# Attention's projections of the second batch and the values placed between the first score blocks, and another order and shape of the stack loads

## The reference, cut to what matters

```python
def _L0_attn_ref(x, w_qkv, w_out, b_out):          # x: (2, 1024, 256)
    qkv = (x @ w_qkv.T).reshape(B, S, 3, H, D)      # H = 16 heads, D = 16
    q, k, v = jnp.moveaxis(qkv, 2, 0)
    ...
    out = _flash_attention_v2(q, k, v, BLOCK_SIZE, scale)   # blocks of 128 keys, their own maxima
    return out.transpose(0, 2, 1, 3).reshape(B, S, E) @ w_out.T + b_out
```

## Time and profile before

| what | value |
|---|---|
| median of 3 runs | 1293.59 us (1291.06 to 1298.01) |
| the profiled execution, its own time | 1297.3 us |
| its span, first to last instruction | 1295.6 us |
| busy PE / DVE / ACT / POOL | 87% / 64% / 49% / 46% |
| mean granted clock of PE | 0.95 of full |
| DMA | 137.21 MB, mean 106 GB/s |

### The profile page before, as it was taken

How to read it: one execution, slowest core, us unless ns; L and a number is a source line. 1 busy time by engine, 2 the same in 40 slices (tenths; PEclk the granted TensorE clock), 3 DMA queues, 4 the chain that set the end, 5 groups by cost and what they waited for, 6 DMA issues and landing times. The chain is left out here.

```text
span 1295.6 us, 21119 instructions
## 1 busy us (share of the span) xinstructions
PE 1128.8 (87%) x6374; PEld 660.5 (51%) x6374; DVE 825.3 (64%) x1537; ACT 633.3 (49%) x1320; POOL 592.2 (46%) x589
## 2 busy tenths in 40 slices
PE   5489999999999995888898977897999998999965
PEld 2152222222222223455753556356888886788854
DVE  6399999999999945665454556897333333222246
ACT  1126777777777781455313342221555554444471
POOL 7000355667345363576541102458544457555521
PEclk8888999999999997999989997899899999999989
DMA  4990234234130104000000000210689888788877
GB/s 135 152 228 14 47 59 64 28 41 61 27 44 13 13 9 171 0 2 1 1 3 1 1 1 10 89 56 26 197 242 242 238 238 252 241 267 255 261 253 253
DMA packets 128383, 137.21 MB, mean 106 GB/s; under 512 B 47430, under 2 KB 99366, under 8 KB 128207
## 3 DMA queue, kind: packets, MB, share of 16 engines
q1 hardware_dynamic: 118783, 110.42, 34.2%
q0 software_dynamic: 9216, 25.18, 6.1%
q10 hardware_dynamic: 272, 0.26, 0.1%
HBM read 109.06 MB, written 24.12 MB: 103 GB/s over the span
## 5 line engine op out<-in xcount | busy, mean ns | idle before, releaser
L495 ACT ACTIVATE l_ret_store<-attn_st 128x512 f32<-128x512 f32 x512 | 280.1, 598 | 103.1 <-PE attn_st L406 93.3
L519 DVE TENSOR_REDUCE attn_neg<-attn_mx 128x8 f32<-128x1024 f32 x256 | 299.2, 1202 | 12.9 <-PE attn_mx L386 11.9
L2010 DVE SCALAR_TENSOR_TENSOR exp_sums<-exp_y_ps,moe_mask,exp_sums 128x256 f32 x159 | 77.0, 484 | 202.8 <-PE exp_y_ps L1921 97.3
L406 PE MATMUL attn_st<-attn_q_st,attn_k_st 128*128 128x512 bf16 x512 | 173.9, 384 | 2.8 <-ACT l_ret_store L495 2.1
L1912 PE MATMUL exp_h_ps<-keep_prod,moe_w 128*88 128x128 f32 x1272 | 169.9, 277 | 7.1 <-DMA moe_w<-in_w 5.2
L386 PE MATMUL attn_mx<-attn_k_st,attn_q_st 96*128 96x512 bf16 x512 | 156.2, 387 | 14.5 <-DVE attn_neg L519 14.2
L1912 PEld LDWEIGHTS exp_h_ps<-keep_prod,moe_w 128*88 128x88 f32 x1272 | 147.8, 158 | 23.6 <-DMA moe_w<-in_w 12.2
L418 PE MATMUL attn_o<-l_ret_store,l_ret_tab 128*32 128x512 f32 x1024 | 136.4, 604 | 0.8 <-ACT l_ret_store L495 0.8
L1874 POOL DMA_INDIRECT y_rows<-exp_sums,moe_dst_i x96 | 93.7, 976 | 82.9 <-DVE exp_sums L2010 75.6
L406 PEld LDWEIGHTS attn_st<-attn_q_st,attn_k_st 128*128 128x128 bf16 x512 | 48.3, 97 | 155.9 <-ACT l_ret_store L495 114.6
L1966 ACT ACTIVATE moe_ht<-exp_h_ps 88x256 f32<-88x256 f32 x159 | 60.4, 380 | 95.6 <-PE exp_h_ps L1912 95.5
(11 more groups left out here) (317 smaller groups left out, 1921.0 us busy)
## 6 DMA issues: line engine op xcount, KB each, us to landing
moe_w<-in_w SPq DMA_DIRECT2D x254, 176.0 KB
keep_prod<-in_w SPq DMA_DIRECT2D x64, 176.0 KB
exp_tiles<-y_rows SPq DMA_DIRECT2D x11, 768.0 KB, 10.3
parts<-l0b_front SPq DMA_DIRECT2D x32, 192.0 KB, 10.6
attn_k_st<-parts SPq DMA_DIRECT2D x48, 128.0 KB, 7.1
attn_q_st<-parts SPq DMA_DIRECT2D x48, 128.0 KB, 7.7
l_ret_tab<-in_tables SPq DMA_DIRECT2D x4, 1024.0 KB
exp_sums<-y_rows SPq DMA_DIRECT2D x5, 768.0 KB, 10.5
```

Of the source, the lines that this page charges most:

```text
L406: pe.matmul(st_ps[n % BANKS][:], k_st[g % BUFS][:, h, kt * P:(kt + 1) * P], q_st[g % BUFS][:, h, c * CH:(c + 1) * CH], start=True, stop=Tr ...
L495: act.activation(probs[s % 2][:, h], st_ps[n % BANKS][:], ACT.Exp, scale=SCALE0).then_inc(exp_done, 1)
L519: dve.tensor_reduce(neg[m % 2][:, i], mx_ps[slot["score", n] % 2][:].rearrange("p (j k) -> p j k", k=P), AX.X, ALU.max, negate=True).then_ ...
L2010: dve.scalar_tensor_tensor(out=sums[:, bass.ds(at, 1)], in0=y_ps[b % 2][:, 0:E].unsqueeze(1), scalar=mask[:, b:b + 1], in1=sums[:, bass.ds ...
```

## The change

Part by part:

1. **PAIRS is reordered**, so that the key parts of the six pairs read 0, 1, 2, 0, 1, 0. RUNS names the three runs of consecutive key parts, and `load_stack` loads them with three transfers of 48, 32 and 16 rows. The columns of `w_qk` are reordered on the host so that a group's 64 channels are ordered dimension by head; a stack row is then one run of 8 KB in DRAM for all four heads. The queries still take six transfers of 16 rows, now after the keys. Nine transfers replace twelve.
2. **Order on PE, DVE and ACT.** Only the eight blocks of batch 0 (EARLY) come first. Then eight rounds follow: scores 2i and 2i+1, block 8+i, values 2i and 2i+1. DVE does two reduces and one split a round. The three banks are dealt in the order of use (`uses`, `bank_of`).
3. **SP's queue.** Stack 0 is loaded after save 4, the copies of the marks go out after save 7, stack 1 after save 9, and stack 2 behind `place_neg(0)`, `place_wj(0)`, x and the bias. `w_v` is loaded by SP after `x_t`, no longer by ACT at the start.
4. **POOL's constants.** The marks are made first, and for one head alone (32 x 1024 instead of 32 x 4096); three transfers spread them over the other heads and stacks instead of two. The memset of `v_st` writes only the half that is not overwritten, and comes later.

The diff, cut:

```diff
-PAIRS = ((0, 0), (0, 1), (1, 0), (1, 1), (0, 2), (2, 0))
+PAIRS = ((0, 0), (0, 1), (0, 2), (1, 0), (1, 1), (2, 0))
+RUNS = ((0, 3), (3, 2), (5, 1))
...
+        EARLY = 8
+        ROUNDS = len(blocks) - EARLY
+        values = [range(NT * i // ROUNDS, NT * (i + 1) // ROUNDS) for i in range(ROUNDS)]
+        uses = [("block", n) for n in range(EARLY)]
+        for i in range(ROUNDS):
+            uses += [("block", EARLY + i)] + [("value", t) for t in values[i]]
+        bank_of = {use: n % BANKS for n, use in enumerate(uses)}
...
+                for j, count in RUNS:
+                    rows = slice(D0 * j, D0 * (j + count))
+                    qp, kp = PAIRS[j]
+                    sp.dma_start(k_st[g % BUFS][rows], a["parts"][g, 1, kp:kp + count].rearrange("a (d h) t -> (a d) h t", h=G0)
+                                 ).then_inc(stack[g % BUFS], 16)
                 for j, (qp, kp) in enumerate(PAIRS):
-                    rows = slice(D0 * j, D0 * j + D0)
-                    sp.dma_start(k_st[g % BUFS][rows], a["parts"][g, 1, kp].rearrange("(h d) t -> d h t", d=D0)
-                                 ).then_inc(stack[g % BUFS], 16)
-                    sp.dma_start(q_st[g % BUFS][rows], a["parts"][g, 0, qp].rearrange("(h d) t -> d h t", d=D0)
+                    sp.dma_start(q_st[g % BUFS][D0 * j:D0 * (j + 1)], a["parts"][g, 0, qp].rearrange("(d h) t -> d h t", h=G0)
                                  ).then_inc(stack[g % BUFS], 16)
...
+            sp.dma_start(w_v[:], a["w_v"].rearrange("(k p) n -> p k n", p=P)).then_inc(v_weights, 16)
             for n in range(len(blocks)):
                 save(n)
-                if n == 3:
+                if n == 4:
                     load_stack(0)
-                if n == 5:
+                if n == EARLY - 1:
+                    sp.wait_ge(ready, 1 + PARTS)
+                    sp.dma_start(k_st[0][STACK:P, 1:G0], k_st[0][STACK:P, 0:1].to_broadcast([P - STACK, G0 - 1, SEQ])
+                                 ).then_inc(marked, 16)
+                    for i in range(1, BUFS):
+                        sp.dma_start(k_st[i][STACK:P], k_st[0][STACK:P, 0:1].to_broadcast([P - STACK, G0, SEQ])
+                                     ).then_inc(marked, 16)
+                if n == EARLY + 1:
                     load_stack(1)
-                if n == 11:
-                    load_stack(2)
-            sp.wait_ge(ready, 10)
-            for i in range(1, BUFS):
-                sp.dma_start(k_st[i][STACK:P], k_st[0][STACK:P]).then_inc(marked, 16)
+            place_neg(0)
+            place_wj(0)
             sp.dma_start(x[:], a["x"].rearrange("(t p) n -> p t n", p=P)).then_inc(x_in, 16)
             sp.dma_start(bias[:], a["b_out"].partition_broadcast(P)).then_inc(x_in, 16)
-            place_neg(0)
-            place_wj(0)
+            load_stack(2)
...
-            ordered(pool.memset(v_st, 1.0))
+            marks = k_st[0][STACK:P, 0].rearrange("r (j k) -> r j k", k=P)
...
+            ordered(pool.memset(v_st.rearrange("p b k h d -> p (b k h) d")[:, :, D0:2 * D0], 1.0))
...
-            for n in range(len(blocks)):
+            for n in range(EARLY):
                 project(n)
             pe.wait_ge(v_weights, 16)
-            for t in range(NT):
-                project_v(t)
-                score(t)
+            for i in range(ROUNDS):
+                score(2 * i)
+                score(2 * i + 1)
+                project(EARLY + i)
+                for t in values[i]:
+                    project_v(t)
...
-            act.dma_start(w_v[:], a["w_v"].rearrange("(k p) n -> p k n", p=P)).then_inc(v_weights, 16)
...
-            for n in range(NB):
+            for n in range(EARLY):
+                split_block(n)
+            for i in range(ROUNDS):
+                reduce(2 * i)
+                reduce(2 * i + 1)
+                split_block(EARLY + i)
```

More of the change, by code:

```diff
@@ L133, in attend @@
         saves = {n: n // SLOTS + 1 for n in range(len(blocks))}
+        EARLY = 8
[5 more added lines that the diff above has]
+        bank_of = {use: n % BANKS for n, use in enumerate(uses)}
+        order_of = {use: n for n, use in enumerate(uses)}
         ring, slot = [], {}
@@ L255, in ordered @@
                 pool.wait_ge(ready, done)
-            ordered(pool.memset(v_st, 1.0))
+            marks = k_st[0][STACK:P, 0].rearrange("r (j k) -> r j k", k=P)
+            ordered(pool.memset(marks, 0.0))
+            for part in range(PARTS):
+                ordered(pool.affine_select(out=marks, in_=marks, compare_op=ALU.not_equal, fill=1.0,
+                                           base=-KTS * part, pattern=[[-1, KTS], [0, P]], channel_multiplier=1))
             for m in (ident_bf, ident):
@@ L347, in _, with free_use @@
         def _(pe):
+            def free_use(kind, n):
+                r = order_of[kind, n] - BANKS
+                if r >= 0:
+                    was, m = uses[r]
+                    pe.wait_ge(rest_done if was == "block" else v_kept, m + 1)
             def project(n):
@@ L358, in project_v @@
             def project_v(t):
-                n = len(blocks) + t
-                if t < BANKS:
-                    pe.wait_ge(rest_done, n - BANKS + 1)
-                else:
-                    pe.wait_ge(v_kept, t - BANKS + 1)
+                free_use("value", t)
                 for k in range(KT):
-                    mm = pe.matmul(st_ps[n % BANKS][:, 0:E], x_t[:, k, t * P:(t + 1) * P], w_v[:, k, :],
+                    mm = pe.matmul(st_ps[bank_of["value", t]][:, 0:E], x_t[:, k, t * P:(t + 1) * P], w_v[:, k, :],
                                    start=(k == 0), stop=(k == KT - 1))
@@ L422, in _ @@
             pe.wait_ge(weights, 16)
[L423 removed]
+            for n in range(EARLY):
                 project(n)
             pe.wait_ge(v_weights, 16)
[L426 to L428 removed]
+            for i in range(ROUNDS):
[4 more added lines that the diff above has]
+                    project_v(t)
+            for n in range(2 * ROUNDS, NB + 2):
+                score(n)
             pe.wait_ge(ready, 11)
[L430 to L431 removed]
             turn_neg(0)
@@ L457, in _ @@
         def _(act):
-            act.dma_start(w_v[:], a["w_v"].rearrange("(k p) n -> p k n", p=P)).then_inc(v_weights, 16)
-            for n in range(len(blocks)):
-                act.wait_ge(projected, n + 1)
-                if n >= SLOTS:
-                    act.wait_ge(saved[n % SLOTS], 32 * saves[n - SLOTS])
-                act.activation(parts[:, n % SLOTS, 0], st_ps[n % BANKS][:], ACT.Copy).then_inc(high_done, 1)
-            act.wait_ge(ready, 1)
-            for t in range(NT):
-                act.wait_ge(v_done, t + 1)
-                act.activation(v_st[:, t // KTS, t % KTS, :, 0:D0],
-                               st_ps[(len(blocks) + t) % BANKS][:, 0:E].rearrange("p (h d) -> p h d", d=D0),
-                               ACT.Copy).then_inc(v_kept, 1)
+            for kind, n in uses:
+                bank = st_ps[bank_of[kind, n]]
+                if kind == "block":
+                    act.wait_ge(projected, n + 1)
+                    if n >= SLOTS:
+                        act.wait_ge(saved[n % SLOTS], 32 * saves[n - SLOTS])
+                    act.activation(parts[:, n % SLOTS, 0], bank[:], ACT.Copy).then_inc(high_done, 1)
+                else:
+                    act.wait_ge(ready, 2 + PARTS + 4)
+                    act.wait_ge(v_done, n + 1)
+                    act.activation(v_st[:, n // KTS, n % KTS, :, 0:D0], bank[:, 0:E].rearrange("p (h d) -> p h d", d=D0),
+                                   ACT.Copy).then_inc(v_kept, 1)
             def keep_neg(m):
@@ L502, in _, with split_block @@
         def _(dve):
-            for n in range(len(blocks)):
+            def split_block(n):
                 dve.wait_ge(high_done, n + 1)
-                dve.tensor_tensor(rest[:, n % 2], st_ps[n % BANKS][:], parts[:, n % SLOTS, 0],
+                dve.tensor_tensor(rest[:, n % 2], st_ps[bank_of["block", n]][:], parts[:, n % SLOTS, 0],
                                   ALU.subtract).then_inc(rest_done, 1)
@@ L544, in invert_total @@
                 dve.reciprocal(total[u % 2][:], total[u % 2][:]).then_inc(inverted, 1)
-            for n in range(NB):
+            for n in range(EARLY):
[4 more added lines that the diff above has]
+                split_block(EARLY + i)
+            for n in range(2 * ROUNDS, NB):
                 reduce(n)
@@ L2120, in lay_out @@
     w = np.asarray(i["L0_attn_w_qkv"])
-    d["w_qk"], d["w_v"] = t(w[:2 * E]), t(w[2 * E:])
+    d["w_qk"], d["w_v"] = t(w[:2 * E].reshape(2 * GROUPS // BATCH, G0, D0, E).swapaxes(1, 2).reshape(2 * E, E)), t(w[2 * E:])
     w = t(np.asarray(i["L0_attn_w_out"])).reshape(KT, 2, G0, D0, E)
```

18 lines of the change are left out of this document (5 added, 13 removed).

## The result

The changed kernel takes 1272.16 us (median of 4 runs, 1270.73 to 1277.06) against 1292.32 before (4 runs, 1287.66 to 1298.01): ratio 0.984, 95% interval 0.9807 to 0.9874. The forecast was 1274.6 with a range of 1269.5 to 1284.5. The profiled span fell from 1295.6 to 1274.1, by 21.5 us.

The account below looks back on a forecast made before the run. DVE bounds attention's loop, so only its start counts: 35.7 + 34.4 + 2.4 + 1.1 + 8.9 = 82.5, 19.0 us earlier than 101.5. From a median of 1293.6 that gives 1274.6 us, range 1269.5 to 1284.5.

Parts of the forecast that it names:

- Bound and rigid rest: Attention's main loop, bound by DVE, and the 837 us behind it move rigidly with the loop's start, 19.0 us earlier.
- Blocks 0 to 3 and POOL: Before the loop: smaller marks on POOL end 10.0 us of DVE stalls; stack 0 issued at 22.9 to 23.0, not 33.2.
- Moving w_v: At the start: w_v no longer shares the DMA with w_qk and the first x_t; 0.5 us taken, bounds 0 to 0.8.
- Stack 0: Stack 0's load: 2.0 us, queries 6.4 and keys 4.3 after issue at 23.0, so scores start at 35.7.
- Rounds: Eight rounds paced by PE at 4.3 us, 34.4 in all, plus 2.4 for PE's restart at its lower clock.
- What hides: Slots for blocks 11 to 15, stack 1 and the marks' transfers are all in time: cost 0.
- the tail of the queue: SP's queue: x, bias and stack 2 finish before place_neg(1) is needed; cost 0, bounds 0 to 3 us.
- D: Rival: PE never gets its full clock in the rounds, loop starts at 114.5, slower than before at 1306.6 us; chance 0.03.
- E: Rival: the rounds stumble on hand-overs between engines, 9.6 us in all, 1284.2 us; chance 0.07.
- C: Rival: place_neg(1) is late behind stack 2 and stops unit 1 by up to 3 us, 1277.6 us; chance 0.08.
- B: Rival: wide transfers bring nothing, keys take 6.4 us, gain 16.9, 1276.7 us; chance 0.13.
- my middle: Time of the keys' three wider transfers taken as 4.3 us, midway between bounds of 6.4 and 2.3.

Follow-up runs that it names:

- keys_then_queries: Kernel before with the new constants and each stack's twelve unchanged transfers sent as six keys, then six queries: 1303.2 us, ratio 0.9924 (kernel before on that chip: 1311.5).
- narrow_keys: Changed kernel with the keys in six transfers of 16 rows instead of three wider ones, 8 KB runs kept: 1273.7 us, ratio 0.9838.
- old_stacks: Changed kernel with six key transfers of 16 rows and the old column order of w_qk (2 KB runs): 1272.8 us, ratio 0.985.
- blocks first: Changed kernel with the old order on PE, ACT and DVE (all 16 blocks before the scores): 1266.0 us, ratio 0.9782.
- values_early: Changed kernel with ten of the sixteen values before the first score: 1273.1 us, ratio 0.9841.
- blocks_first_old_queue: Changed kernel with the old order on PE, ACT and DVE and the old order of SP's queue: 1274.5 us, ratio 0.9864.
- old_queue: Changed kernel with the old order of SP's queue: 1279.2 us, ratio 0.9907.

## Why the prediction was right, point by point

- **Bound and rigid rest.** Right. The loop and what follows move with the loop's start: 20.3 us at its first product, 20.7 at the last exponential, 21.5 in the span, 20.2 in the medians. Forecast 19.0. The difference of 1 to 2 us is about what two executions of the same instructions differ by at their start.
- **Blocks 0 to 3 and POOL.** Right: stack 0's first transfer at 23.06 for a forecast of 22.9 to 23.0. That it is so close is luck: in the other executions with the same instructions ahead of it, it lies between 21.65 and 23.21. The 10.0 us read as DVE standing beside POOL's selects came back as 10.0 to 10.2 when the constants were taken back. Moving w_v: ACT's first copy lies at 10.26 to 10.84 in the executions with w_v behind x_t and at 11.04 to 11.27 in the three with w_v at the start, about the 0.5 us taken; at block 1 the scatter covers it.
- **Stack 0.** First score 35.0 for 35.7, by two errors that nearly cancel, so partly luck. I took the old stack, 14.8 us with its 2.0, as the price of 16-row transfers and let only the keys' width shorten it, by 2.1 us. Width gives 0.9 to 1.3. The other part is one that I did not see: twelve narrow transfers are slower when those of keys and queries alternate, and the change ended that; block 10 came 1.8 us earlier by it. 14.8 less 1.8 and 1.1 is 11.9, and 12.0 were measured. "The queries are the same six transfers of 16 rows: 6.4 us at 123 GB/s" is the step that does not hold: keys_then_queries shows 135 and 142 GB/s for unchanged transfers. (The 123 itself has saves in its last microsecond; from 36 to 47 us it is 117.) The Trainium skill ("SBUF — State Buffer", Door 1: The DMA port swizzle) gives the transfer of 16 partitions about 104 GB/s, and its section "Can I just issue two DMAs to hit both halves?" says that two concurrent transfers, at partitions 0 and 64, gain 6% over one. The trace is near the first, 13% above it (118), and goes beyond the second with its many narrow transfers (14 to 20% more).
- **Rounds.** 4.31 us for 4.3, first round 6.7 for 4.3 + 2.4. find_least at 72.78 for 73.6. Right.
- **What hides, and the tail of the queue.** Right: no copy on ACT waits for a save in the changed kernel. Stack 2's last transfer had been issued at 90.6, and `place_neg(1)` went out at 100.72 without holding PE: PE waits at most 0.9 us for those maxima in both kernels.
- **Rivals.** D did not come: PE ran 30.0 of the 30 us from 42 to 72 at 1.00. The Trainium skill's rule on cycling through PSUM banks ("TensorE: Matmul & The Clock Gate", A second HAM failure mode: psum-queue depth-cycling) does not show here. E did not come. C did not come. B and my middle share the truth: B had the wide transfers bring nothing and I 2.1 us, and they brought 0.9 to 1.3 at the first score; at the times, narrow_keys and old_stacks cannot be told from the changed kernel.
- **What the text implied and the runs refute.** I wrote that the scores "stand behind all 16 blocks in PE's list", as if their early start were the gain. It is not: starting scores at 35 instead of 44 us costs 6 to 7 us, since DVE has 16 splits and 24 reduces to do before the loop in any order (16 x 1.78 + 24 x 1.2 = 57 us), and what counts is when DVE stands idle. The changed kernel leaves it idle from 26.7 to 36.1 and paces the rounds by PE; blocks first does not. The number came out right because I summed the order as it stands, and never asked what the old order would give with the other edits.

## What to carry to other kernels

When a change has four parts, forecast each alone as well as the sum: here constants and queue gained about 11 and 8 us, and the part named first lost 6 to 7. Before comparing places of single executions, look how far an early instruction that all of them share is apart. In a phase that one engine bounds, count that engine's work before the phase's end and look for its idle stretches; starting a later stage early is worth nothing if work that could have run in the wait is postponed for it. And look at what two neighbouring DMA transfers write: the order of transfers in a queue is a parameter like their width.

## What the runs showed of the hardware

- Stack data flowed at 118 GB/s when each two transfers in a row wrote the same 16 partitions (of two different tensors), and at 135 and 142 GB/s when the keys went first, so that the next one wrote other partitions; transfers, sizes and runs of 2 KB were the same. What about the order does it was not separated.
- Runs of 8 KB instead of 2 KB in DRAM changed nothing that could be seen at 16 rows a transfer (13.3 and 12.9 us to the first score).
- PE's clock after a wait: 1.00 in the round after a wait of 1.41 us, 0.72 after 2.46, 0.64 after 11.32, in the same instructions. In values_early, whose first round has no values, it is 0.60 after 2.61.
- SP's issue of the bias behind x's 2 MB took 8.09 us, 7.33 in blocks_first_old_queue, 3.79 in old_queue, and 2.05 in the changed kernel:

```profile
83.02 2.05 SPq L236 DMA_DIRECT2D attn_bias<-in_b_out  x1
```

x's transfer stands ahead of it in all four, so what else is queued seems to decide how long SP is held; that was not tried by itself. place_neg(0), where it stands behind the bias in SP's list, is held as well.
